# Attention scores on four 64x64 tiles of TensorE, the values one step later, and a bias in one operation: one change to an attention and mixture-of-experts kernel

## What is computed

```
x = x + xattn(layernorm(x), ctx, ctx, mask)      # 16 heads of 8, softmax over 64 keys
x = x + moe(layernorm(x))                        # 16 experts of 64, top 2, and a shared expert of 128

scores = einsum('bhqd,bhkd->bhqk', qh, kh) / scale
scores = where(mask, NEG_INF, scores)
attn   = softmax(scores);  ctx = attn @ vh;  out = ctx @ Wo.T
```

## Time and profile before

| what | value |
|---|---|
| median of 3 runs | 190.49 us |
| the profiled execution | 190.56 us |
| its span, first to last instruction | 188.7 us |
| mean granted TensorE clock | 0.985 |
| busy: TensorE, VectorE, ScalarE, GpSimd | 92%, 85%, 69%, 47% |

### The profile page before, as it was taken

The page is one execution under the profiler, slowest core; times in us unless marked ns, Lnnn a source line. Parts: engine busy times, 40 slices in busy tenths (PEclk is TensorE's granted clock), DMA queues, the critical chain, the costliest instruction groups (busy, mean ns, idle before and its releaser), DMA issues.

```text
span 188.7 us, 4275 instructions
## 1 busy us (share of the span) xinstructions
PE 173.1 (92%) x1305; PEld 124.9 (66%) x1305; DVE 161.4 (85%) x501; ACT 130.2 (69%) x292; POOL 89.2 (47%) x146
## 2 busy tenths in 40 slices
PE   7887889787999999999999799999999999999963
PEld 7763455455666666666677476788878877788741
DVE  5569999997999999999984899988988899889961
ACT  3195797776899999999889566565556555665631
POOL 7049997369888888888698850400000000000000
PEclk9999999999999999999999999999999999999985
DMA  5999200000000000000003423432534153315201
GB/s 105 288 332 386 96 2 2 3 0 2 3 0 5 0 0 0 0 0 5 0 1 94 147 106 109 118 115 92 152 118 154 70 158 136 130 63 161 62 2 56
DMA packets 12128, 15.43 MB, mean 82 GB/s; under 512 B 1744, under 2 KB 6608, under 8 KB 11984
## 3 DMA queue, kind: packets, MB, share of 16 engines
q1 hardware_dynamic: 10800, 13.79, 22.8%
q10 hardware_dynamic: 1312, 1.46, 2.8%
HBM read 14.06 MB, written 1.18 MB: 81 GB/s over the span
## 4 chain that ended last, share of the span: by engine, by line
PE 55%; DVE 23%; issue 7%; ACT 4%; DMA 4%; POOL 3%; ACTq 1%; DVEq 0%; POOLq 0%
PE bank L1092 31%; PE bank L1039 8%; PE bank L1021 4%; DMA mhalf<-mask_half 4%; PE bank L1030 4%; DVE hid L904 4%; DVE smax L827 4%; DVE prob L848 3%; ACT hid_hi L667 2%; DVE k_all L769 2%; PE bank L1010 2%; PE bank L1000 2%; DVE stats L701 1%; POOL k_blk L455 1%; PE bank L990 1%
## 5 line engine op out<-in xcount | busy, mean ns | idle before, releaser
L1039 PE MATMUL bank<-k_blk,q_blk 128*128 128x512 f32 x64 | 33.9, 614 | 1.3 <-POOL k_blk L455 1.1
L658 ACT ACTIVATE sig<-bank 128x512 f32<-128x512 f32 x36 | 21.5, 599 | 19.1 <-PE bank L1092 18.7
L455 POOL TENSOR_TENSOR k_blk<-k_all,consts_sb 128x512 f32<-128x512 f32 x32 | 33.2, 1058 | 0.0
L667 ACT CAST hid_hi<-hid 128x512 fp32r<-128x512 f32 (+1 forms) x37 | 22.4, 609 | 12.0 <-DVE hid L904 11.9
L1092 PE MATMUL bank<-xt_hi,w_hi 128*128 (+1 forms) x72 | 29.3, 407 | 0.2 <-ACT sig L658 0.2
L896 DVE TENSOR_TENSOR hid_lo<-hid,hid_hi 128x512 fp32r<-128x512 f32 (+1 forms) x37 | 25.1, 680 | 4.3 <-ACT hid_hi L667 4.1
L1092 PE MATMUL bank<-xt_hi,w_lo 128*128 (+1 forms) x72 | 28.2, 392 | 0.0
L1092 PE MATMUL bank<-xt_lo,w_hi 128*128 (+1 forms) x72 | 28.2, 392 | 0.0
L602 ACT ACTIVATE prob<-prob,exp_scale 128x512 f32<-128x512 f32 x32 | 23.8, 744 | 2.9 <-DVE prob L848 2.9
L887 DVE TENSOR_TENSOR hid_u<-sig,bank 128x512 f32<-128x512 f32 x32 | 21.8, 682 | 3.9 <-PE bank L1092 2.5
L904 DVE TENSOR_TENSOR hid<-hid_u,cb 128x512 f32<-128x512 f32 x32 | 23.0, 718 | 0.0
(11 more groups left out here) (117 smaller groups left out, 333.2 us busy)
## 6 DMA issues: line engine op xcount, KB each, us to landing
cb<-comb_rows SPq DMA_DIRECT2D x64, 128.0 KB, 2.9
w_moe_sb<-w_moe SPq DMA_DIRECT2D x1, 1296.0 KB, 10.3
ctxt_sb<-ctx_t SPq DMA_DIRECT2D x4, 256.0 KB, 8.7
xt_sb<-x_t ACTq DMA_DIRECT2D x4, 256.0 KB, 8.4
x_sb<-x SPq DMA_DIRECT2D x4, 256.0 KB, 11.0
out<-x_sb SPq DMA_DIRECT2D x3, 256.0 KB, 3.1
w_moe_sb<-w_moe SPq DMA_DIRECT2D x1, 432.0 KB, 7.9
w_att_sb<-w_att SPq DMA_DIRECT2D x1, 264.0 KB, 3.9
```

The source lines that it names most:

```text
L455: last = nc.gpsimd.tensor_tensor(k_blk[p][:, g, :, :], k_all[:, bass.ds(t, 1), g, :].broadcast_to([P, HG, S]), hmask_sb.rearrange("p (h o) ...
L658: nc.scalar.activation(sig[r][:, :], gate_ps[r][:, :], ACT.Silu).then_inc(s_sig, 1)
L667: nc.scalar.copy(hid_hi[k][:, cols], hid[k][:, cols]).then_inc(s_hid_hi, 1)
L1039: nc.tensor.matmul(score_ps[g][:, :], q_blk[q][:, g, :, :].rearrange("p b s -> p (b s)"), k_blk[q][:, g, :, :].rearrange("p h s -> p (h s) ...
```

## The change

- The scores become four products of 64 rows and 64 columns: one for each sequence b (rows of the array, `q_blk` and `k_blk` partitions 64b on) and head half hg (columns, output partitions 64hg on). Bank b now holds sequence b with (head half, query) as partitions; before, bank g held head half g with (sequence, query). `q_blk` needs no zeros and is half as large; GpSimd copies it by multiplying with ones.
- `exp_scale` becomes two tiles, one for each b, whose partitions are written by four operations of 64 rows for a group of tiles, with two waits of GpSimd on itself.
- TensorE: scores of tile t+2 stand at the end of step t behind router(t-2), and wait for both subtractions of tile t+1; before they stood in step t+1. All values of tile t-1 stand at the start of step t, before transposes(0); before, values of t stood at the end of step t. The second head block's place is gone; attention_transposed stands behind norm_transposed.
- ScalarE: `pvt_sb` of tile t-1 stands ahead of copy 0; att_t behind copy 1; `v_blk` of tile t is made in step t, not in t-1; the exponentials stand together at the end.
- VectorE: reciprocal and attention stand between subtraction 0 and maximum 1; the negated mean (819) is gone.
- GpSimd: bias2 = mean * rstd * -1 by one `tensor_scalar` with two scalars.

```diff
-        exp_scale = sb("exp_scale", [P, TILES])
+        exp_scale = [sb(f"exp_scale{b}", [P, TILES]) for b in range(BPT)]
+        ones_sb = sb("ones_sb", [P, S])
-        q_blk = [sb(f"q_blk{p}", [P, 2, BPT, S]) for p in range(2)]
+        q_blk = [sb(f"q_blk{p}", [P, 2, S]) for p in range(2)]
...
-                nc.gpsimd.tensor_tensor(exp_scale[:, tiles], rstd1[p][:, :], any_scale[:, tiles],
-                                        ALU.mult).then_inc(s_escale, 1)
+                for turned in range(2):
+                    for b in range(BPT):
+                        src = slice(b * S, (b + 1) * S)
+                        hg = 1 - b if turned else b
+                        last = nc.gpsimd.tensor_tensor(exp_scale[b][hg * S:(hg + 1) * S, tiles], rstd1[p][src, :],
+                                                       any_scale[src, tiles], ALU.mult)
+                    last.then_inc(s_escale, 1)
+                    pool.wait_ge(s_escale, 2 * g + turned + 1)
...
-                nc.gpsimd.tensor_tensor(
-                    q_blk[p][:, :, :, :],
...
+                nc.gpsimd.tensor_tensor(q_blk[p][:, :, :], q,
+                                        ones_sb[:, :].rearrange("p (o s) -> p o s", o=1).broadcast_to([P, 2, S]),
+                                        ALU.mult)
...
-                    pool.wait_ge(s_nmean2, t - 1)
-                    nc.gpsimd.tensor_tensor(bias2[p][:, :], neg_mean2[p][:, :], rstd2[p][:, :], ALU.mult).then_inc(s_bias2, 1)
+                    nc.gpsimd.tensor_scalar(bias2[p][:, :], mv2[p][:, 0:1], rstd2[p][:, 0:1], -1.0, ALU.mult,
+                                            ALU.mult).then_inc(s_bias2, 1)
...
+                if on(1) and not (isinstance(t, int) and t == TILES):
+                    values_to_sbuf(t - 1)
                 if on(0):
                     transposed(0)
...
+                if on(0):
+                    transposed(1)
                 if on(1):
                     act.wait_ge(s_at, t)
                     nc.scalar.copy(att_t[q][:, :], at_ps[:, 0:P]).then_inc(s_at_sb, 1)
-                if on(0):
-                    transposed(1)
...
+                if on(1) and not on(-1):
+                    attention()
                 if on(-1):
                     for g in range(2):
                         if g == 1:
+                            if on(1):
+                                attention()
                             row_max(1)
...
+                def scores(n, r):
+                    if once and n == 0:
+                        pe.wait_ge(s_blk_first, 1)
+                    else:
+                        pe.wait_ge(s_const, 16)
                         for b in range(BPT):
+                            pe.wait_ge(s_sub[b], n)
+                    for b in range(BPT):
+                        rows = slice(b * S, (b + 1) * S)
+                        for hg in range(2):
+                            last = nc.tensor.matmul(score_ps[b][hg * S:(hg + 1) * S, :], q_blk[r][rows, hg, :],
+                                                    k_blk[r][rows, hg, :, :].rearrange("p h s -> p (h s)"), start=True,
+                                                    stop=True, tile_position=(b * S, hg * S))
+                        last.then_inc(s_score[b], 1)
...
                 if on(1):
...
+                    values(t - 1, q)
                 if on(0):
                     transposes(0)
...
+                    values_as_rows(t - 1)
                 if on(0):
                     transposes(1)
                 if on(2):
                     norm_transposed(t - 2, p)
                 if on(1):
...
+                    attention_transposed(t - 1, q)
                     output_projection(t - 1, q)
...
+                if on(-2) and not (once and t < 0):
+                    pe.wait_ge(s_blk, t + 2)
                 if on(2):
                     router(t - 2, p)
+                if on(-2) and not (once and t < 0):
+                    scores(t + 2, p)
```

More of the change, by code:

```diff
@@ L458, in k_blocks @@
                         hmask_sb.rearrange("p (h o) -> p h o", o=1).broadcast_to([P, HG, S]), ALU.mult)
-                last.then_inc(s_blk, 1)
+                last.then_inc(written, 1)
             mask_ctx(1)
@@ L622, in step, with values_to_sbuf @@
                     exponentials(0)
-                if on(0):
-                    act.wait_ge(s_pvt, t + 1)
-                    nc.scalar.copy(pvt_sb[:, :], pvt_ps).then_inc(s_pvt_sb, 1)
-                if on(-1):
                     exponentials(1)
+            def values_to_sbuf(t):
+                act.wait_ge(s_pvt, t + 1)
+                nc.scalar.copy(pvt_sb[:, :], pvt_ps).then_inc(s_pvt_sb, 1)
             def weights_to_sbuf(half):
@@ L680, in _ @@
             pipeline(act, step)
+            values_to_sbuf(TILES - 1)
             silu(0, 0)
@@ L984, in keys_values, with values @@
                 last.then_inc(s_v, 1)
+            def values(t, p):
+                pe.wait_ge(s_vblk, t + 1)
+                for h in range(2):
+                    pe.wait_ge(s_pt_sb[h], t + 1)
+                    for hg in range(2):
+                        for c in range(GT):
+                            last = nc.tensor.matmul(
+                                pvt_ps[c * PW:(c + 1) * PW, hg * P + h * S:hg * P + (h + 1) * S],
+                                v_blk[p][:, h, hg * GT + c, :], prob_t[p][:, h * GT + c, hg * S:(hg + 1) * S],
+                                start=True, stop=True, tile_position=(0, c * PW))
+                last.then_inc(s_pvt, 1)
             def values_as_rows(t):
@@ L1022, in transposes @@
                     last.then_inc(s_pt[h], 1)
[L1024 to L1046 removed]
+                def scores(n, r):
[3 more added lines that the diff above has]
+                        pe.wait_ge(s_const, 16)
+                        for b in range(BPT):
+                            pe.wait_ge(s_sub[b], n)
+                    for b in range(BPT):
+                        rows = slice(b * S, (b + 1) * S)
+                        for hg in range(2):
+                            last = nc.tensor.matmul(score_ps[b][hg * S:(hg + 1) * S, :], q_blk[r][rows, hg, :],
+                                                    k_blk[r][rows, hg, :, :].rearrange("p h s -> p (h s)"), start=True,
+                                                    stop=True, tile_position=(b * S, hg * S))
+                        last.then_inc(s_score[b], 1)
+                if once and t < 1:
+                    if t == 0:
+                        pe.wait_ge(s_blk, 1)
+                    scores(t + 1, q)
+                elif not on(-1):
                     pe.wait_ge(s_sub[0], TILES)
@@ L1049, in step @@
                     weights_as_rows(0)
+                if once and t == 0:
+                    pe.wait_ge(s_k_raw, GROUPS - 1)
                 if on(1):
@@ L1054, in step @@
                         pe.wait_ge(s_k_raw, GROUPS)
-                    values_as_rows(t - 1)
+                    values(t - 1, q)
                 if on(0):
                     transposes(0)
-                if on(-1):
-                    scores(1)
-                else:
+                if not on(-1):
                     pe.wait_ge(s_sub[1], TILES)
@@ L1063, in step @@
                 if on(1):
-                    if once and t == TILES - 1:
-                        pe.wait_ge(s_ct_sb, 1)
-                    attention_transposed(t - 1, q)
+                    values_as_rows(t - 1)
                 if on(0):
@@ L1152, in _ @@
             pipeline(pe, step)
+            values(TILES - 1, 1)
             gate(0, 1)
```

71 lines of the change are left out of this document (21 added, 50 removed).

## The result

The changed kernel takes 197.53 us (median of 4 runs, 196.94 to 198.31), the kernel before 190.50: a ratio of 1.039, 95% interval 1.033 to 1.045. Slower by 7.0 us, where +3.1 was forecast and "within 2%" held the largest chance. The profiled execution took 196.94 us with a span of 195.0, against 190.56 and 188.7.

What follows compares the result with a forecast made beforehand. TensorE was taken to bound the 4.52 us steps, VectorE 0.3 us behind. Start-up +1.0, loop +1.65 and end +0.5 summed to +3.15 us on the profiled 190.56, giving 193.6 us by the median; range 189.0 to 200.0.

Steps and rivals of the forecast that it cites:

- (a): Score products on TensorE: four quarters run beside one another, 1.00 us of columns instead of 1.72.
- rival C: Scores: row halves don't run beside each other, 0.86 us more a step, 203 us; chance 0.07.
- first-in-first-out form: Scores: nothing on a tile is reordered, so only neighbours overlap, 2.14 us a score stage, 207.6 us; chance 0.03.
- (b): TensorE's changes of tile shape: 0.1 us each, three a step instead of two, +0.1 us.
- (c): Values one step later on TensorE: 0.50 us instead of 0.72; TensorE in sum 3.5 us a step.
- (e): New loop: each step a round trip TensorE - ScalarE - TensorE, 4.72 us against 4.52, +0.20 us a step.
- (f): GpSimd's work and start-up: exp_scale +0.65 us, bias 0.19; tile 5's last subtraction at 50.6 us, +1.0 us.
- Rival D: GpSimd's 64-row or two-scalar operations cost 1 us each, start-up +3 more, 196.6 us; chance 0.10.
- (g): Tile 5's last subtraction to tile 15's: ten steps of 4.72 us and 0.8 of extras, 48.0 us, +1.65 us.
- (h): Behind tile 15: delayed values while expert products fill TensorE, 0 to +1 us, taken as +0.5.
- rival B: Loop: not slower, VectorE stays the bound, 4.43 us a step, 190.1 us (188.5 with an end gain); chance 0.20.
- Rival E: Loop: faster by over 2%, at least 0.4 us a step of TensorE's spared time comes out, 186.5 us; chance 0.04.

Runs made afterwards that it cites:

- e_xn_first: Changed kernel with ScalarE's xn ahead of its first copy of transposed scores; 196.9 us, ratio 1.033.
- e_clock2: Changed kernel with 3, 5 and 12 unread extra TensorE products in steps 1 to 3; 195.38 us, ratio 1.030.
- b_dve_load: Kernel before with one more unread 128x128 VectorE addition behind the first maximum of each step; 193.92 us, ratio 1.023.
- e_full_array: Changed kernel's new order with the old whole-array score products, q block and exp_scale; 204.59 us, ratio 1.072.
- e_tiles_alone: Kernel before with the score tiles at its first score product's place, an unread 4-column product carrying the waits; 194.38 us, ratio 1.024.
- e_tiles_nodummy: Kernel before with the score tiles, no 4-column product, both waits a step earlier ahead of the router; 193.89 us, ratio 1.021.
- e_both: Changed kernel with xn ahead of the first copy and 3, 5 and 12 unread TensorE products in steps 1 to 3; 194.46 us, ratio 1.024.
- e_clock: Changed kernel with 2, 4 and 5 unread extra TensorE products in steps 1 to 3; 196.9 us, ratio 1.030.

## Why the prediction was right and wrong

What held. (a): 1.00 us of columns and 1.15 to 1.2 us for the 8 records were forecast, 1.09 came; rival C (halves of the rows in turn, from 1.1 us up, 203 us) and its first-in-first-out form (207.6) are out. The Trainium skill ("TensorE: Matmul & The Clock Gate", Part 3) has matmuls strictly first in, first out in start and end. 8 records of 0.43 us of columns in 1.09 us don't fit the form that I made of it, so the two records of a product don't hold back the neighbouring tile. The same part of the Trainium skill models the span of packed tiles as one matmul and about 4 ns for each further tile. The trace agrees: a record of 0.61 us, the second one 0.43 later and three further tiles make 1.06 us (an estimate), and 1.09 came. One reading there was loose: of the value products two of a column quarter stand together in program order, as four records, not four products. (b) and (c): values at S + 1.02 (forecast 1.10). (e), as a mechanism: with S = 57.91, copy 1 stands at 2.30 (2.34), xn at 2.78 (2.82), copy 2 at 3.18 (3.19), att_t at 3.81 (3.82), xt_hi and projection at 4.12 (4.12), and VectorE's last subtraction at 3.86 (3.91); e_xn_first then moved the step by the 0.15 us that this chain says. (f), as far as GpSimd goes: tile 5's scores at 46.59, forecast 46.7. The four exp_scale operations take 0.98 us in all, forecast 0.65 more than 0.20 = 0.85; the two-scalar bias takes 0.26 us and a wait of 0.17 on its own rstd, 0.19 was taken, and the cover named for it held. Rival D, 1 us each, is out.

What failed. Of the 3.15 us that the sum falls short of the span's +6.3, 1.3 lie in (f), 1.5 in (g) and 0.4 in (h). The causes, in the order of size:

1. **No step of the prediction looked at the clock.** (f) put tile 5's last subtraction at S + 3.91 = 50.6 us; it came at 51.88, S + 5.29, for the most part because the scores themselves took 0.77 us longer and the values 0.43. A round trip in which TensorE idles 1.2 us was written down, and the waits of the start-up, without the question what the chip makes of an idle TensorE: a term put at nothing without a reason. By e_clock2 this is 1.57 us of the profiled difference. What in the changed kernel brings the clock down stays open, since the kernel before waits there as well.

2. **Term (e), +0.20 us a step, was mis-sized: +0.33.** The last two links were short: the router was taken 0.05 us behind the end of xt_hi, at 4.45, and came 0.15 behind it, at 4.55; router to scores was taken as 0.27 and was 0.30. Ten steps of 0.33 are 3.3 instead of 2.0, and (g) measured +3.15 instead of +1.65.

3. **The baseline of (e) and of rival B.** "TensorE bounds these steps, but VectorE is only 0.3 us behind it" took both limits from busy times. b_dve_load shows that the round trip through VectorE had no slack at all, and the step that doesn't wait for it is 4.49 us, so the two were level within about 0.03 us. This made the gain look spendable: 0.83 us a step of TensorE's work really goes (e_full_array against the changed kernel), and in the new order none of it came out (4.85). Rival E needed VectorE's rows to shrink; they didn't (4.40 us a step against 4.24). Rival B's 4.43 us was not reached in any version; its nearest is the 4.45 estimated from e_tiles_alone and e_tiles_nodummy, which no run has.

4. **Term (h), +0.5, was +0.86.** From tile 15's scores to the expert stage it is 24.78 us instead of 22.99, and part of this comes back behind it. Its parts I followed only to two places, tile 14's values behind the first gate product and GpSimd's casts of w_lo, which TensorE waits for 0.4 to 0.5 us; no run isolates them.

Open is the tail. Also open is whether another order of ScalarE's copies would bring e_both's 4.70 back to 4.52. No run tried one, and its timeline speaks against it as long as att doesn't come earlier too: att_t could have started 0.03 us sooner at most. The chance of "slower" was 0.39, because the likeliest case's sum ended 0.7 us under the border of 2%, and that sum held only the waits that had been found: the clock and every link taken short could only add. The range reached to 200.0, over every case but C, and none of its cases had the clock: that it holds the measured 197.53 us is luck as far as those 1.57 us go.

## What to carry to other kernels

An engine that is busy all of a step isn't thereby its only bound. The records of products reached some 0.17 us beyond their columns here, and waits hid under that; and a round trip through another engine was level with TensorE's work. Put a small useless operation on the next engine and see whether the step moves, before work is taken off the first. Small array tiles make a product shorter, but they may ask for another order of the work: price the order by itself, with the old products in the new places, since here it cost more (1.16 us a step) than the tiles gave (0.83). And when work is taken from TensorE or waits are added to it, read the granted clock of the stretches that have the longest waits, and count them at the lower level in the forecast.

## What was unexpected of the hardware

- The clock fell in a kernel whose TensorE is still mostly busy. In the windows of 2 us from 38 to 40 and 44 to 46 it is busy 1.72 and 0.86 us, with single idle stretches of no more than 1.3 us, and 0.50 is granted in 40 to 42 and 48 to 50. The Trainium skill ("TensorE: Matmul & The Clock Gate", Part 1, on a second failure mode) tells of a kernel whose TensorE idles briefly but often between groups of matmuls, and whose clock swings between its two levels. The trace of the changed kernel agrees, with stretches of 1.04 and 1.23 us; that of the kernel before, with 1.03, 0.81 and 0.98 us in the same steps, keeps 1.00.
- Added work makes it faster: 5 products on TensorE in step 3 left 6.30 us from tile 5's scores to tile 6's, 12 left 4.91. And where another engine's wait hides TensorE (tiles 4 to 5, 7.50 us with the clock at 0.50 for a part of it, 7.61 and 7.49 at the full level in e_clock and e_clock2), a fall of the clock costs nothing.
- Eight records of 512 columns on four 64x64 tiles take 1.09 us from first start to last end, four on the whole array 1.96, so the 2 by 2 split costs 0.11 us over half of the time.
- A GpSimd operation on 64 partitions and 4 elements takes 0.20 us, as the 128x4 one before, and four of them with their waits 0.98: it is the number of operations that counts there.
